# Packed 16-head attention: value products in runs of four units a unit later, small jobs in the units of runs, maxima 18 units in advance

## What is computed

```
def _L0_xattn_ref(q, k, v, Wq, bq, Wk, bk, Wv, bv, Wo, bo):
    qh = proj(q, Wq, bq)
    kh = proj(k, Wk, bk)
    vh = proj(v, Wv, bv)
    scores = jnp.einsum('bhqd,bhkd->bhqk', qh, kh) / jnp.sqrt(jnp.asarray(D_K, jnp.float32))
    attn = jax.nn.softmax(scores, axis=-1)
    out = jnp.einsum('bhqk,bhkd->bhqd', attn, vh)
    concat = out.transpose(0, 2, 1, 3).reshape(bs, -1, D_MODEL)
    return concat @ Wo.T + bo
x = x + jnp.tanh(g_xattn[0]) * _L0_xattn_ref(_layernorm(x, axis=-1), ctx_1024, ctx_1024, ...)
```

## Time and profile before

| | us |
|---|---|
| median of 3 runs | 5828.71 (5826.62 to 5843.3) |
| the profiled execution | 5833.64 |
| its span | 5831.9 |
| TensorE busy in the span | 5276.3 (90%) |
| VectorE busy | 3851.6 (66%) |
| ScalarE busy | 3100.1 (53%) |
| GpSimd busy | 1589.2 (27%) |

### The profile page before, as it was taken

One profiled execution on the slowest core, in us unless ns is written; L12 is line 12 of the kernel. 1 busy time (PEld: TensorE's weight loads), 2 busy tenths in 40 slices (PEclk: granted clock), 3 DMA queues, 4 the chain that ended last, 5 costly groups with the idle time before them and its releaser, 6 DMA issues. The chain is left out here.

```text
span 5831.9 us, 109941 instructions
## 1 busy us (share of the span) xinstructions
PE 5276.3 (90%) x39878; PEld 3466.6 (59%) x39878; DVE 3851.6 (66%) x10948; ACT 3100.1 (53%) x4492; POOL 1589.2 (27%) x1360
## 2 busy tenths in 40 slices
PE   6999999997959999999999988979458999999996
PEld 4666666665835555555555547857355666666663
DVE  5666666665766766766766657756466676767674
ACT  3666666664624444444444445634145666666664
POOL 3222222221442222222222214500352222222220
PEclk9999999998979999999999998989578999999998
DMA  3323333332233323333332315479223232323230
GB/s 86 77 67 77 70 75 78 71 72 60 58 87 91 82 72 78 82 76 74 82 79 71 82 40 108 77 198 252 82 91 77 68 76 67 77 67 78 67 72 13
DMA packets 160603, 475.40 MB, mean 82 GB/s; under 512 B 34721, under 2 KB 85724, under 8 KB 159867
## 3 DMA queue, kind: packets, MB, share of 16 engines
q1 hardware_dynamic: 148738, 449.69, 32.5%
q0 software_dynamic: 11328, 18.72, 1.1%
HBM read 237.66 MB, written 19.88 MB: 44 GB/s over the span
## 5 line engine op out<-in xcount | busy, mean ns | idle before, releaser
L692 DVE CUSTOM_DVE_ANT_0 a_dump<-a_max,a_mqf 100x482 f32<-100x482 f32 (+1 forms) x1536 | 978.5, 657 | 426.5 <-PE a_max L883 395.6
L1635 PE MATMUL a_max<-a_stack,a_qblk 96*128 96x482 f32 (+1 forms) x2304 | 1030.4, 449 | 28.7 <-DMA a_stack<-a_khi 17.6
L1473 DVE CUSTOM_DVE_ANT_0 a_dump<-a_max,a_penq 128x482 f32<-128x482 f32 (+3 forms) x1248 | 783.0, 655 | 409.1 <-PE a_max L1635 386.9
L1466 DVE TENSOR_REDUCE a_mx<-a_max 128x1 f32<-128x482 f32 (+3 forms) x1248 | 779.6, 654 | 406.6 <-PE a_max L1635 283.4
L565 ACT ACTIVATE a_probs<-a_scores 128x800 f32<-128x800 f32 (+1 forms) x768 | 643.2, 838 | 657.4 <-PE a_scores L900 657.2
L1368 ACT ACTIVATE a_probs<-a_scores,a_kbias 128x800 f32<-128x800 f32 (+1 forms) x768 | 697.3, 926 | 404.1 <-PE a_scores L1662 404.1
L1662 PE MATMUL a_scores<-a_qblk,a_stack 128*128 128x400 f32 (+1 forms) x3072 | 832.9, 353 | 40.6 <-POOL a_qblk L1283 34.0
L1370 ACT ACTIVATE a_probs<-a_scores 128x800 f32<-128x800 f32 (+1 forms) x768 | 624.7, 836 | 410.0 <-PE a_scores L1662 406.0
L883 PE MATMUL a_max<-a_stack,a_qblk 96*100 96x482 f32 (+1 forms) x1536 | 712.1, 485 | 39.5 <-DVE a_mx L692 27.6
L1674 PE MATMUL a_pv<-a_probs,a_v_aug 128*32 128x200 f32 x12288 | 705.7, 341 | 3.0 <-ACT a_probs L1368 2.1
L1662 PEld LDWEIGHTS a_scores<-a_qblk,a_stack 128*128 128x128 f32 (+1 forms) x3072 | 548.3, 184 | 185.0 <-POOL a_qblk L1283 57.6
(11 more groups left out here) (554 smaller groups left out, 8473.0 us busy)
## 6 DMA issues: line engine op xcount, KB each, us to landing
a_stack<-a_khi SPq DMA_DIRECT2D x768, 180.5 KB, 3.3
a_ctxT<-in_ctxT_dram SPq DMA_DIRECT2D x128, 722.0 KB, 14.3
a_stack<-a_klo SPq DMA_DIRECT2D x384, 180.5 KB, 3.5
f_wb<-weights_by_token SPq DMA_DIRECT2D x16, 1600.0 KB
a_ctxn<-in_ctxn_dram SPq DMA_DIRECT2D x32, 704.0 KB
a_mt_i<-in_mask1T_dram SPq DMA_DIRECT2D x32, 600.0 KB, 6.9
a_mq_i<-in_mask_dram SPq DMA_DIRECT2D x32, 564.1 KB
a_mask_i<-in_mask_dram SPq DMA_DIRECT2D x32, 541.5 KB
```

The lines of the kernel that those rows point to most:

```text
L692: nc.vector.tensor_tensor_reduce(dump[:, k % 2, 0:n], src, mqf[:, b % 2, o:o + n], 1.0, -3.0e38, ALU.mult, ALU.max, out_).then_inc(mx_free, 1)
L1466: nc.vector.tensor_reduce(out_, src, AX.X, ALU.max).then_inc(mx_free, 1)
L1473: nc.vector.tensor_tensor_reduce(dump[0:rows, k % 2, 0:n], src, penq[0:rows, b % 2, o:o + n], 1.0, -3.0e38, ALU.add, ALU.max, out_).then_i ...
L1635: pe.matmul(to[:, 0:n], qblk[0:96, b % 2, at:at + D], stack[0:96, b % 2, g, o:o + n], start=True, stop=True).then_inc(mx_full, 1)
```

## The change

- `PACKED_UNITS` = 18 takes the place of 16 for these two phases: the maxima run 27 jobs ahead, not 24, and the prologue makes three more.
- `TOGETHER` = 4: value products stand in runs of four units, in units 1, 5, 9, ..., 21, and take the units from five to two before (before: in even units those of the two before). `probs` has six buffers.
- `out`, `concat`, `wo` go from units 2, 5, 8 to 5, 9, 13, the query projection from 18 to 17, `left` from 8, 12, 16 to 9, 13, 17. Negations and key and value projections stay.
- ScalarE copies the finished value sums a unit later (ahead of the exponentials of units 2 and 14), and the query in unit 19.

```diff
--- before.py
+++ after.py
@@ -1009,9 +1009,10 @@
 PACKED = 3
 LEFT = 4 * S - PACKED * D
 MAX_JOBS = 2 * PACKED * NCH
-PACKED_LEAD = 3 * LEAD // 2
-LEFT_AT = (8, 12, 16)
-TOGETHER = 2
+PACKED_UNITS = 18
+PACKED_LEAD = 3 * PACKED_UNITS // 2
+LEFT_AT = (9, 13, 17)
+TOGETHER = 4
 
 
 def packed_attention_phase(nc, name, x, xnT, ident, w, dram, scale, gate, lens=None):
@@ -1105,7 +1106,7 @@
         LOADED = 16 * len(loads)
         CONSTS = 8 + (1 if lens is not None else 0)
 
-        OUT_AT, CONCAT_AT, WO_AT, NEG1_AT, Q_AT, NEG0_AT = 2, 5, 8, 9, 18, 21
+        OUT_AT, CONCAT_AT, WO_AT, NEG1_AT, Q_AT, NEG0_AT = 5, 9, 13, 9, 17, 21
         V01_AT, V2_AT, K0_AT, K12_AT = 9, 11, 13, 15
         K0_FIRST, K12_FIRST, Q_FIRST, LEFT_FIRST, NEG_FIRST = 5, 8, 10, 12, 15
 
@@ -1135,7 +1136,7 @@
             if job is not None:
                 take(mx_turn, job)
 
-        for g in range(LEAD):
+        for g in range(PACKED_UNITS):
             for k in range(3 * g // 2, 3 * (g + 1) // 2):
                 take_max(job_of(k))
             if g == LEFT_FIRST:
@@ -1380,9 +1381,9 @@
             q_round(1)
             for b in range(B):
                 for u in range(UNITS):
-                    if u == 1 and b > 0:
+                    if u == 2 and b > 0:
                         pv_evac(b - 1, 1)
-                    if u == KT + 1:
+                    if u == KT + 2:
                         pv_evac(b, 0)
                     if u == Q_AT + 2 and b + 2 < B:
                         q_round(b + 2)
@@ -1740,8 +1741,8 @@
                         neg_turn(b + 1, 0)
                     for k in fulls[1:]:
                         max_mm(job_of(k))
-                    if u % TOGETHER == 0 and (b > 0 or u > 0):
-                        for back in range(TOGETHER, 0, -1):
+                    if u % TOGETHER == 1 and (b > 0 or u > 1):
+                        for back in range(TOGETHER + 1, 1, -1):
                             at = UNITS * b + u - back
                             pv_mm(at // UNITS, at % UNITS)
                     left_mm(left_of(b, u))
```

## The result

The changed kernel takes 5941.89 us (median of 4 runs, 5938.5 to 5945.16), the kernel before 5830.93 (4 runs, 5826.62 to 5843.3): 1.0187 of the time before, 95% interval 1.0169 to 1.0204. It is slower by 111 us; 98 were forecast, within a range of 5850 to 5985 us for the time itself. The profiled execution took 5938.89 us, its span is 5937.1.

A forecast was written before the change was run, and what follows sets the result against it. TensorE's program order was taken as the bound, other engines hidden. Savings of 3.3 us a batch in a0 and 4.8 in a3 stood against new waits of 4.9 and 7.0; walked batch lengths gave +98 us, 5927 us, range 5850 to 5985.

The forecast's parts named there:

- Runs of four at 0.34 a unit: Value products on TensorE: a run of four takes 1.50 us, 1.70 with edges, against 2.03; saves 2.0 us a batch.
- The wait for POOL goes: TensorE's wait for POOL's q block disappears, saving 0.8 us a batch in a0 and 0.9 in a3.
- In a3 the wait of value products for exponentials goes: In a3 this wait and some 0.2 us on concat disappear, saving 1.4 us a batch.
- Small jobs share the run's entering switch, 0.1 each: Query, negation and output products directly ahead of a run save 0.1 us each, five a batch, 0.5 us.
- Score-buffer waits, 2.1 us in units 14 to 17: Scores and k12 wait for two buffers read by ScalarE: 0.45, 0.35 and 1.3 us; 2.1 in a0, 1.9 in a3.
- the walk: Timing of each stretch between runs against buffers; new waits a batch sum to 4.9 us in a0, 7.0 in a3.
- VectorE's ring, units 18 to 21 and 2 to 9: Three maxima buffers wait for VectorE: a0 1.0 us in 18 to 21, 0.9 in 2 to 9; a3 1.4 and 2.2.
- The lengths: Run-to-run stretches sum to batches of 42.3 us in a0 against 40.80 and 43.6 in a3 against 41.83.
- The lead: Maxima running two units earlier, with three more in the prologue (1.7 us a stage) and three fewer last, cost nothing.
- Rival 1: VectorE's reductions don't bind, only score-buffer waits remain; each pair of batches gains 2.6 us: 5749 us, chance 0.08.
- rival 2: No change: waits come to 8.1 us a pair because several fall on one another; 5829 us, chance 0.06.
- rival 3: Much slower: long runs pace at 0.41, or late units delay VectorE's next stretch; 5980 to 6005 us, chance 0.07.

The follow-up runs named there:

- short_copy: The changed kernel with ScalarE copying only 60 of each 480 or 482 columns of the k0 and k12 projections from the third batch on; 0.9993 of the time before.
- short_reduce: The changed kernel with VectorE reducing only 240 of the 480 or 482 columns of each maximum product; 1.0009 of the time before.
- lead_only: The kernel before with only the longer lead: 18 units in the prologue loops, 27 maximum jobs in advance; 1.0067 of the time before.
- lead16: The changed kernel with the maxima 16 units in advance, as before (PACKED_UNITS = 16); 1.0254 of the time before.

## Why the prediction was right

- **Runs of four at 0.34 a unit**: right. 1.50 us for 32 records; the bound of 0.41 falls.
- **The wait for POOL goes**: right, none is left.
- **In a3 the wait of value products for exponentials goes**: right in effect. 12.2 us over 38 waits of this kind are still listed, but the runs of units 1 and 5 start 0.46 and 0.90 us behind the score product in a3 as in a0.
- **Small jobs share the run's entering switch, 0.1 each**: too small for the negations, which run beside the value products (0.01 to the run's first record). For the other small jobs it wasn't taken apart.
- **Score-buffer waits, 2.1 us in units 14 to 17**: right in mechanism and size. From due time to start: score of 15 0.43 (0.45 forecast), `k12` 0.59 (0.35), score of 17 1.24 (1.3). The 0.2 too little at `k12` is ScalarE's copy of the value sums, which the change puts ahead of the exponential of 14 and which the walk had left out. Units 10 to 13: 0.31 and 0.37, forecast 0.3 and 0.3. short_copy shows the cause.
- **VectorE's ring, units 18 to 21 and 2 to 9**: right in place. In units 18 to 21 0.21, 0.49 and 0.33 us wait, 1.0 forecast; the first of them, the third maximum waiting for `left`'s buffer, was not in the walk. In units 6 to 9 0.32 ahead of the sixth maximum (0.4 forecast) and 0.26 ahead of the negation (0.5; it starts 0.44 behind `concat`, and 0.18 in short_reduce).
- **The lengths**, from the first maximum behind a run to the next such one: in the batch shown of a0 4.86, 5.11, 8.19, 8.22, 10.46 and 5.70, 42.5 in all; the walk's 4.6 + 5.0 + 8.4 + 8.2 + 10.0 + 5.8 + 0.3 gave 42.3. In a3, mean of the middle batches, 5.04, 6.20, 8.44, 7.94, 10.19 and 6.04, 43.85 in all, for 4.8 + 6.1 + 8.9 + 7.7 + 9.7 + 6.1 + 0.3 = 43.6. The sum was short by 0.15 and 0.25 us a batch, 12 us over both stages, which is the 98 for 111. It is so near partly by luck: units 14 to 17 were 0.5 too short in both stages and units 6 to 9 too long, 0.2 in a0 and 0.5 in a3.
- **The lead**: taken at nothing. It isn't nothing, but depends on the runs: +0.67% alone, -0.67% here.
- **Rival 1** (VectorE's reductions don't bind) falls by short_reduce, **rival 2** (no change) by the measured time, **rival 3** (a slower pace in long runs) by the trace.
- The Trainium skill's rule in "TensorEngine Tiling (Array Packing)", PSUM Bottleneck, says that copies out of PSUM may become the bound once tiling has quickened the matmuls. Here readers of PSUM do become the bound, as short_copy and short_reduce show, but by another way than the rule's: what they read are the products of projections and maxima, which aren't column-tiled (128*128 and 96*128) and got no faster, and no wait of TensorE names the copy of the tiled value sums. The prediction called the rule its own mechanism; its walk was about cover and buffers, and it is the walk that held.

What stays open: the shortened kernels give back 113 and 104 us, each singly; both shortenings in one kernel were not run, so whether they add up isn't known. The walk had 369 us of new waits; these two account for some 217 of them at most, the copies of `v01` and `v2` and the plain stretches' exponentials are seen in the rows alone, and what short_reduce leaves of the ring's cost was only argued. Of the savings, the run's edges stand in the rows, but no kernel shows all of them at once: with most waits covered, runs of four brought 0.5 us a batch over runs of two in a0, not 2.0.

## What to carry to other kernels

A bound engine's work is also the cover of the engines that read its results. Before gathering a kind of work into longer runs, list what is then left bare between the runs, and follow each small ring of buffers through one burst: the reader's duration times the jobs, against the number of buffers. If a run is to stay long, put the jobs with long copies directly ahead of it; and measure the run's length again after that, since the same kernel wanted four units in the stage where the exponential takes 0.84 us and two where it takes 0.93. (That the exponential alone makes this difference between the stages wasn't tried.)

## What the runs showed of the hardware

- A cast of 7 columns by VectorE, 0.17 us else, took 1.39 us when it began during a GpSimd operation on SBUF (lead_only), and ended 0.03 us behind it, as 61 of 61 did. In lead16 60 casts met POOL's shorter operation on the query and took 0.30 to 0.41 us. The Trainium skill, "SBUF — State Buffer", section "SBUF: two separate sides", says that a VectorE instruction which needs the port pair shared with GpSimd (one in a two-port mode, for instance) and a GpSimd instruction exclude each other for the whole instruction, whichever began first; the ends of these casts agree, though no run here shows the cast's mode. So a move of two units in one engine's list can cost 0.7% by meeting another engine's long operation.
- A 32-column matmul and value products on other column groups ran at once (642.91 to 643.11), and the run's first record came 0.01 us behind the negation's, without the 0.09 us that entering a run costs otherwise.
